# A mixer kernel in which TensorE's waits stand one product earlier, and two small blocks of other engines move

## What is computed

```python
x = x + mamba2(xn) + ffn(xn)
# mamba2: proj = xn @ in_proj_w.T            -> gate (8192), hs|B|C (8192+1024+1024), dt (128)
#         hs,B,C = silu(conv1d_4taps(...)+b) ; dt = softplus(dt+bias); A_cs = cumsum(-exp(A_log)*dt)
#         Y_diag = ((C B^T) * exp(segsum)) @ (hs*dt)        per 128-token chunk and head
#         states = B^T @ (hs*dt*decay), carried from chunk to chunk
#         Y_off  = (C @ prev_states) * exp(A_cs);  y = Y_diag + Y_off + D*hs
#         y*silu(gate), normalised by group of 1024 channels, @ out_proj_w.T
# ffn:    xn @ W.T + b + a low-rank term whose rank (8,16,32,64) a softmax picks per token
```

## Time and profile before

| | us |
|---|---|
| median of 3 runs | 1581.26 (1580.66 to 1581.79) |
| the profiled execution's own time | 1580.66 |
| its span in the profile | 1578.9 |
| busy: PE, DVE, ACT, POOL | 1559.5, 1414.5, 1367.7, 1291.1 |
| mean granted TensorE clock | 1.0 of full speed |

### The profile page before, as it was taken

The page is one execution under the profiler, slowest core; times in us unless marked ns, Lnnn a source line. Parts: engine busy times, 40 slices in busy tenths (PEclk is TensorE's granted clock), DMA queues, the critical chain, the costliest instruction groups (busy, mean ns, idle before and its releaser), DMA issues.

```text
span 1578.9 us, 29209 instructions
## 1 busy us (share of the span) xinstructions
PE 1559.5 (99%) x9172; PEld 1271.9 (81%) x9172; DVE 1414.5 (90%) x2343; ACT 1367.7 (87%) x2620; POOL 1291.1 (82%) x1614
## 2 busy tenths in 40 slices
PE   8999999999999999999999999999999999999998
PEld 7877888888888888887778788888888888888886
DVE  6988999999999999999979898898898888888887
ACT  4678899999999999989846899999999999999996
POOL 5549998999999998989874488778787878787786
PEclk9999999999999999999999999999999999999999
DMA  5257767676776676766614666766667667667673
GB/s 178 94 171 223 197 214 221 196 226 195 220 225 198 213 224 199 220 202 208 198 42 142 201 198 222 218 201 225 212 200 230 200 210 222 199 221 215 202 225 92
DMA packets 231754, 311.83 MB, mean 197 GB/s; under 512 B 144176, under 2 KB 160560, under 8 KB 231344
## 3 DMA queue, kind: packets, MB, share of 16 engines
q1 hardware_dynamic: 231600, 309.97, 63.9%
HBM read 240.69 MB, written 36.70 MB: 176 GB/s over the span
## 4 chain that ended last, share of the span: by engine, by line
PE 87%; DVE 5%; POOL 4%; issue 2%; ACT 1%; DMA 1%; SPq 0%; DVEq 0%; ACTq 0%; POOLq 0%
PE bg L804 21%; PE bo L975 20%; PE bt L804 12%; PE bh L804 11%; PE by L1031 7%; PE bg L1053 7%; PE bt L1018 3%; PE bh L1018 2%; PE bo L783 1%; POOL wl L631 1%; DVE cv L1085 1%; PE bo L862 1%; POOL xl L734 1%; DMA turned<-tg 1%; POOL wol L750 1%
## 5 line engine op out<-in xcount | busy, mean ns | idle before, releaser
L407 ACT ACTIVATE mt<-cs_row,cs_tok 128x128 f32<-128x128 f32 x1024 | 324.5, 390 | 0.0
L631 POOL TENSOR_TENSOR wl<-raw,wh 128x256 fp32r<-128x256 f32 x328 | 250.2, 792 | 59.1 <-ACT wh L379 59.1
L725 POOL COPY xt<-turned 128x512 uint16<-128x512 uint16 x248 | 202.3, 862 | 42.3 <-DMA turned<-tg 42.3
L716 POOL TENSOR_TENSOR mt<-mt,gt 128x256 f32<-128x256 f32 x128 | 118.0, 943 | 141.7 <-ACT mt L588 141.2
L741 POOL TENSOR_TENSOR sqa<-sqa,sq 128x256 f32<-128x256 f32 x222 | 223.7, 1027 | 1.0 <-ACT sq L561 1.0
L750 POOL TENSOR_TENSOR wol<-raw_o,woh 128x256 fp32r<-128x256 f32 x256 | 190.4, 764 | 10.5 <-ACT woh L528 10.5
L734 POOL TENSOR_TENSOR xl<-xg,xh 128x256 fp32r<-128x256 f32 x254 | 189.7, 768 | 6.0 <-ACT xh L541 6.0
L1085 DVE SCALAR_TENSOR_TENSOR cv<-bt,par_sb,cv 128x511 f32<-128x511 f32 (+2 forms) x192 | 143.7, 748 | 49.3 <-ACT cv L383 44.8
L1085 DVE SCALAR_TENSOR_TENSOR cv<-bh,par_sb,cv 128x511 f32<-128x511 f32 (+2 forms) x192 | 143.7, 748 | 35.4 <-ACT cv L383 30.9
L379 ACT ACTIVATE wh<-raw 128x1024 fp32r<-128x1024 f32 (+1 forms) x146 | 152.3, 1043 | 0.7 <-DMA raw<-in_w_dtag 0.7
L975 PE MATMUL bo<-woh,xl 128*128 128x512 f32 x508 | 149.1, 415 | 0.4 <-POOL xl L734 0.4
(11 more groups left out here) (215 smaller groups left out, 3814.7 us busy)
## 6 DMA issues: line engine op xcount, KB each, us to landing
raw<-in_w_step SPq DMA_DIRECT2D x128, 512.0 KB, 4.6
cs_row<-cs_rows SPq DMA_DIRECT2D x128, 512.0 KB, 7.0
low_parts<-wl SPq DMA_DIRECT2D x64, 512.0 KB, 5.8
raw_o<-in_w_out SPq DMA_DIRECT2D x128, 256.0 KB, 5.7
wl<-low_parts SPq DMA_DIRECT2D x64, 512.0 KB, 4.7
ec_row<-ec_rows SPq DMA_DIRECT2D x256, 96.0 KB, 5.7
raw<-in_w_bc SPq DMA_DIRECT2D x16, 512.0 KB, 3.6
acc<-in_x SPq DMA_DIRECT2D x8, 256.0 KB, 5.4
```

The lines of the kernel that those rows point to most:

```text
L407: e = act.activation(mt[:, m % 2, h, chunk(j)], cs_row[:, m % 2, h, chunk(j)], ACT.Relu, bias=cs_tok[:, j, 2 * m + h:2 * m + h + 1], scale ...
L631: e = pool.tensor_tensor(wl[:, n % 2, cols], raw[:, n % 2, cols], wh[:, n % 2, cols].bitcast(F32), ALU.subtract)
L725: e = pool.tensor_copy(to[:, half], turned[:, NJ * half:NJ * (half + 1), :])
```

## The change

**TensorE.** With `early_state`, the waits of five kinds move to stand before the last product of the kind ahead: what the states need is awaited before the fourth `wol,xh` product; the third output part's `p_xl` before the last state product; what the chunk products need before the fourth `woh,xl` product; what the sum of squares and the carried part's first product need before the eighth chunk product; the next projection's `a_wh` before the last product of the carried part. Among the carried part's needs is the second `v_s`, so its second product now waits for the fourth.

**POOL.** `add_bias` leaves iterations 2 to 5 of the loop and stands behind `split_lo` of the groups g = 4 to 7; its first call awaits `p_lo` too.

**DVE.** The second batch's statistics and norms stand ahead of the step's taps.

The core of the diff:

```diff
                 if j == 0:
                     pool.wait_ge(ld_wb, 48)
+                    pool.wait_ge(p_lo, b + 1)
                     pool.wait_ge(pv, b * PRO_DVE + PRO_DVE_LORA)
...
                     if g == 3:
                         add_ffn(b)
+                    if g >= GROUPS - NJ:
+                        add_bias(b, g - (GROUPS - NJ))
...
-                    if 2 <= m < 2 + NJ:
-                        add_bias(b, m - 2)
...
+                    def await_states():
+                        pe.wait_ge(v_xd, did(n - 1))
+                        if not by_dma(b, m - 1):
+                            pe.wait_ge(v_x, did(n - 1))
+                        if m > 2 and (m - 2) % PER_GROUP == 0:
+                            pe.wait_ge(v_ms, did((n - 2) // PER_GROUP - 1))
+                        if m == 1:
+                            pe.wait_ge(a_bt, did(b * GROUPS + (GROUPS - 1)))
+
+                    def await_chunks():
+                        pe.wait_ge(v_x, did(n - 1))
+                        pe.wait_ge(v_m, did(n - 1))
+                        if b + 1 == NB:
+                            pe.wait_ge(p_m, m)
+                        if bank_y(b, m - 1) is by:
+                            pe.wait_ge(v_xg, did(n - 2))
+
+                    def await_squares():
+                        pe.wait_ge(v_h2, did(un))
+                        pe.wait_ge(p_sqa, squares(b, m - 2))
+
+                    def await_off():
+                        pe.wait_ge(v_sg, did(min(n, b * STEPS + STEPS - 1)))
+                        pe.wait_ge(v_off, did(n - 2))
+                        pe.wait_ge(a_s1, did(n - 1))
+                        pe.wait_ge(v_s, did(n - 1, 4, 2))
...
                                 for j in range(NJ):
+                                    if then and k == ks[-1] and j == NJ - 1:
+                                        then()
...
-                            output(range(2) if early_state else range(3))
+                            if early_state:
+                                output(range(2), await_states)
+                            else:
+                                output()
...
                         for c in range(NS):
+                            if early_state and c == NS - 1:
+                                pe.wait_ge(p_xl, did(n - 2))
...
                         if early_state:
-                            output((2,))
...
+                            output((2,), await_chunks, awaited=True)
+                        else:
+                            await_chunks()
                         for j in range(NJ):
                             for h in range(2):
+                                if early_state and j == NJ - 1 and h == 1:
+                                    if ends:
+                                        await_squares()
+                                    await_off()
...
+                            if c == 1:
+                                pe.wait_ge(v_s, did(n - 1, 4, 4))
+                            if c == NS - 1 and early_state and has(m + 1):
+                                await_weights(b, step(b, m + 1))
...
+                    if b + 1 < NB and STEPS - 12 <= m < STEPS - 6:
+                        h, part_of = divmod(m - (STEPS - 12), 3)
+                        if part_of < 2:
+                            stats_of(b + 1, 2 * h + part_of)
+                        else:
+                            variance(b + 1, h)
+                    if b + 1 < NB and STEPS - NJ <= m < STEPS:
+                        norm(b + 1, m - (STEPS - NJ))
                     if has(m):
                         for k in range(1, TAPS):
                             tap(n, un, u, mine, k)
```

More of the change, by code:

```diff
@@ L791, in tokens, with await_weights, project @@
                 return lambda k: t[:, b, k, :] if j is None else t[:, b, k, chunk(j)]
-            def project(dst, b, n, kind):
+            def await_weights(b, n):
                 pe.wait_ge(a_wh, did(n))
+            def project(dst, b, n, kind, awaited=False):
+                if not awaited:
+                    await_weights(b, n)
                 for i, (w, t) in enumerate(((wh, xTh), (wh, xTl), (wl, xTh))):
@@ L934, in sum_squares, with output @@
                         return mm
-                    def output(ks=range(3)):
+                    def await_states():
[21 more added lines that the diff above has]
+                        pe.wait_ge(v_s, did(n - 1, 4, 2))
+                    def output(ks=range(3), then=None, awaited=False):
                         first, very_last = (m - 2) % PER_GROUP == 0, n - 2 == NB * STEPS - 1
@@ L970, in output @@
                                 a, c = parts[k]
-                                wait_low(k)
+                                if not awaited:
+                                    wait_low(k)
                                 for j in range(NJ):
+                                    if then and k == ks[-1] and j == NJ - 1:
+                                        then()
                                     if k == 0:
@@ L982, in _ @@
                             pe.wait_ge(v_h2, did(un - 4 + m))
-                        project(mine, b, step(b, m), 0).then_inc(t_hs, 1)
+                        project(mine, b, step(b, m), 0, awaited=m > 2).then_inc(t_hs, 1)
                         if m == 0:
@@ L1034, in _ @@
                     if ends and m < STEPS:
-                        pe.wait_ge(v_h2, did(un))
-                        pe.wait_ge(p_sqa, squares(b, m - 2))
                         sum_squares(mine, sqa).then_inc(t_ss, 1)
@@ L1045, in _ @@
                     if has(m - 1):
-                        pe.wait_ge(v_sg, did(min(n, b * STEPS + STEPS - 1)))
-                        pe.wait_ge(v_off, did(n - 2))
+                        if not early_state:
+                            await_off()
                         for c in range(NS):
-                            if c == 0:
-                                pe.wait_ge(a_s1, did(n - 1))
-                            else:
-                                pe.wait_ge(v_s, did(n - 1, 4, 2 * c))
+                            if c == 1:
+                                pe.wait_ge(v_s, did(n - 1, 4, 4))
+                            if c == NS - 1 and early_state and has(m + 1):
+                                await_weights(b, step(b, m + 1))
                             mm = pe.matmul(bg[:, chunk(c)], S[:, c, :], ct[:, g, chunk(c + 1)], start=True, stop=True)
@@ L1361, in _ @@
                             mask_scores(b, GROUPS - 1)
-                    if b + 1 < NB and STEPS - 12 <= m < STEPS - 6:
-                        h, part_of = divmod(m - (STEPS - 12), 3)
-                        if part_of < 2:
-                            stats_of(b + 1, 2 * h + part_of)
-                        else:
-                            variance(b + 1, h)
-                    if b + 1 < NB and STEPS - NJ <= m < STEPS:
-                        norm(b + 1, m - (STEPS - NJ))
                     if has(m - 1):
```

17 lines of the change are left out of this document (3 added, 14 removed).

## The result

The changed kernel takes 1605.32 us (median of 4 runs, 1603.2 to 1605.96), the kernel before 1581.06 (4 runs, 1580.66 to 1581.79): ratio 1.015, 95% interval 1.0134 to 1.0167, 24 us slower. The sign held, and the time lies in the prediction's wide range (1574 to 1608, for 8 in 10). It lies outside the band around its forecast of 1594 (1588 to 1601): the loss is nearly twice the 13 us of its sum.

A forecast was written before the change was run, and what follows sets the result against it. The prediction took TensorE to bound the kernel (PE busy 1559.5 of 1578.9 us). Its terms, 7.8 + 3.3 + 5.3 - 2.1 - 1.2 = +13.1 us on 1580.66, gave 1594 us, with 1574 to 1608 for 8 in 10.

The forecast's parts named there:

- early wait for `xd`: Wait moved before the fourth `wol,xh` product: load late, partly covered; 7.8 us in batch 0, 3.3 us in batch 1.
- early wait for `v_s`: Wait moved before the eighth chunk product: 2.0 us plus 3.3 us, sum 5.3 us, with ends of 1 and 16.
- bias and statistics: POOL's bias moved to later groups, -2.1 us; DVE's statistics moved ahead of the taps, -2.8 us.
- norm before the taps: Iteration 60, DVE: the norm waits for POOL's first `rstd`, `xd` comes 2.66 us later; +1.6 us.
- the met waits: TensorE's early `p_xl`, `v_x`, squares' waits and `a_wh`: already met when reached, so they cost nothing.
- the two gaps at the change of width: Idle "issue" before chunk (45.5 us) and carried loads (21.5 us) stays; rival blaming the waits: 1557 us, chance 0.12.
- `xd` in an ordinary step of batch 0: Fourth `wol,xh` load 0.19 us late, 0.12 free; about 0.10 us lost in each of about 46 steps.
- the step on `v_s` before the eighth chunk product: Second state sum ends 0.01 us before the last chunk load, 0.06 needed; 0.05 us for 40 steps, 2.0 us.
- the 0.10 us of credit in batch 0: The `xd` stall comes after `t_g`, so its 0.10 us was to cover the need of `v_s` in batch 0.
- a group's second step: TensorE meets DVE's late state sums one product sooner: 0.26 us more in 7 steps of batch 1.
- `xd` in batch 0: Early `xd` wait: 46 steps at 0.10 us and 14 at the full 0.23 us, 7.8 us together.
- The rival of the freed DVE: TensorE's slower pace shifts POOL's work out of `xd`'s way; `xd` terms fall to about 2 us: 1583.4, chance 0.15.

## Why the prediction came out as it did

| term, us | forecast | measured | from |
|---|---|---|---|
| early wait for `xd` | +11.1 | +7.5 | 1590.09 - 1582.58 |
| early wait for `v_s` | +5.3 | +15.2 | 1605.32 - 1590.09 |
| bias and statistics | -4.9 | -3.5 | 1577.89 - 1581.35 |
| norm before the taps | +1.6 | +3.5 | 1582.58 - 1579.06 |
| the met waits | 0 | +1.2, not told from 0 | 1579.06 - 1577.89 |

The differences hold in this order only, and each is uncertain by some 2 us. Without the wait for `xd`, the one for `v_s` costs 20.7 us (1603.32 - 1582.58), for then nothing covers part of it. The two together cost 22.7 us, and the forecast for them was 16.4. That is 6.3 of the missing 11 us; the norm, the smaller gain of bias and statistics and the met waits are the rest.

**What held.** The bound and the mechanism: TensorE sets the pace, the two gaps at the change of width do not come from the waits, and each early wait costs what it is late, less what is covered. The rule of the Trainium skill (TensorEngine Tiling (Array Packing), Key Properties), that a change of tiling mode drains TensorE, agrees with the rows: in the kernel before, the changed one and the two with met waits alone they have 45.5 to 47.1 us of "issue" at the chunk loads and 21.5 to 22.5 at the carried part's, whichever waits stood there. `xd` in an ordinary step of batch 0 was right to the hundredth: 0.22 lost, 0.12 given back; and in batch 1 the version with `v_s` late again pays 3.3 to 3.5 us, forecast 3.3. By the starts of the states' loads the bias gave 2.0 us up to the sixth, forecast 2.1, and the statistics 2.9 from the 52nd to the 59th, forecast 2.8; the medians show 3.5 of these 4.9, which their spread allows.

**What failed: the step on `v_s` before the eighth chunk product.** The prediction set the second sum's end (1127.24) against the last chunk load (1127.25) and took 0.05 us for 40 steps. Three things were wrong in it. The wait sits on the first of the product's two loads, which runs at 1127.14, beside the seventh product's. The release takes 0.10 us, not 0.06, as four semaphores meet there. Then the load is 1127.24 + 0.11 - 1127.14 = 0.21 us late, of which 0.05 is covered: 0.16, the measured 0.157. Against the kernel before, a step of batch 1 is 0.166 us longer (10.946, before 10.780). Third, the 0.10 us of credit in batch 0 did not cover the need: without the `xd` stall the chunk loads are 0.21 us longer there, the stall covers 0.11, and 0.10 is left to pay in each step. The prediction had 5.3 us for all of `v_s`. By the starts of the states' loads the changed kernel takes 7.5 us more than the one with `v_s` late again in the first 58 steps of batch 0 and 7.1 in batch 1. In batch 1 an ordinary step pays 0.09 net, as the 0.07 of `xd` goes away at the same time, and a group's second step 0.38 (11.15 to 11.53), where the prediction had 0.26. The prediction named both of the first two ("if the four semaphores need an extra instruction and the wait reaches the first of the product's two loads") and gave 16 us as the upper end, but took a value near the lower one. The row with four loads in 0.25 us, which shows the pairs, stood in the same trace.

**`xd` in batch 0** was put too high, and this hid part of the error on `v_s`. The forecast was 7.8 us, of which 3.2 for 14 steps at the full 0.23: the second and third of each group. With `v_s` late again, against the version with only met waits, the first 58 steps take 3.7 us more, and the 23 of them at the starts of groups only 0.6 together, though TensorE waits for `xd` there in both. So such a step did not lose the 0.23; why not, no run here settles. The 7.5 us of the table also hold 1.3 us around iteration 60, where one profile has 6.8 us at half clock and the other 3.4.

**The norm** was forecast to delay `xd` by 2.66 us and to cost 1.6. DVE stood 2.66 instead of 2.2, and `xd` behind it took 1.10 us instead of 0.55, since it met other work of POOL than before. And the sum had no term for the clock, which fell to half for 3.4 us behind the wait.

**The rival of the freed DVE** was half right: in batch 1 `xd` fell from 772 to 603 ns, and its term there vanished. But the time did not fall, since the stall that freed it cost more. That rival's sum puts the `v_s` term at 4 where the text has 5.3; with 5.3 it gives 1584.7 and not 1583.4.

## What to carry to other kernels

Before a wait is moved ahead, set the end of what it waits for against the start of the very instruction that will carry it, the first load of the product, in a window narrow enough to part loads that run in pairs. Add the release time, which depends on how many semaphores meet there: a late one is worth keeping apart from met ones. A met wait cost nothing in any place tried here, so moving it brought nothing; and a stall may show only as longer busy time of a group, never as a wait. Where an engine stands for microseconds, look at the granted clock behind it too.

## What the hardware showed that I had not expected

**`xd` finishes 0.41 us after a POOL instruction.** POOL's subtraction for `xl`, two instructions, and DVE's `xd` in four kernels, batch 1. The kernel before:

```profile
1122.51 1.45 POOL L734 TENSOR_TENSOR xl<-xg,xh 128x256 fp32r<-128x256 f32 x2
1123.56 0.81 DVE L1299 TENSOR_TENSOR xd<-xt,dd_tok 128x384 f32<-128x384 f32 x1
```

The changed one:

```profile
1117.76 1.43 POOL L737 TENSOR_TENSOR xl<-xg,xh 128x256 fp32r<-128x256 f32 x2
...
1119.01 0.60 DVE L1333 TENSOR_TENSOR xd<-xt,dd_tok 128x384 f32<-128x384 f32 x1
```

The one with the state sums awaited late:

```profile
1130.61 1.44 POOL L737 TENSOR_TENSOR xl<-xg,xh 128x256 fp32r<-128x256 f32 x2
1131.49 0.97 DVE L1336 TENSOR_TENSOR xd<-xt,dd_tok 128x384 f32<-128x384 f32 x1
```

The one with the state copy first:

```profile
1112.62 1.44 POOL L737 TENSOR_TENSOR xl<-xg,xh 128x256 fp32r<-128x256 f32 x2
1113.62 0.85 DVE L1333 TENSOR_TENSOR xd<-xt,dd_tok 128x384 f32<-128x384 f32 x1
```

`xd` lies beside the end of `xl` for 0.40, 0.18, 0.56 and 0.44 us, and lasts 0.81, 0.60, 0.97 and 0.85: the difference is 0.41 or 0.42 each time. POOL's other work does the same. In batch 0 nearly half of them begin beside the sum of squares (L741) instead and end 0.42 us after the end of its first instruction. In the fourteen profiles, from 150 us to 1575 us, 1622 of 1709 `xd` end between 0.400 and 0.425 us after the end of some POOL instruction. The other 87 all last 0.545 to 0.557 us, the least there is. So what one shape takes here, from 0.55 to 1.19 us, goes with where in POOL's work `xd` begins. The Trainium skill (SBUF — State Buffer, SBUF: two separate sides) describes such a lock, held for a whole instruction; the rows agree. No run here moved POOL's work alone.

**The granted clock can fall behind a wait.** Eight of these kernels have the norm ahead of the taps with a late `rstd`. In the profiles of seven of them TensorE's loads stand 2.5 to 4.1 us for `xd` of iteration 60, and the granted clock is 0.5 for 3.4 or 6.8 us, from within the wait or from up to 1.2 us behind it; in the eighth they stand 3.2 us and it stays at 1.0. None of the six other kernels has such a stretch. With the state sums awaited late again, the one execution with a mean granted clock of 1.0 took 1586.02 us, the four with 0.998 took 1589.49 to 1591.15.

**Two products with 64 weight columns load together.** Their loads start in pairs, 0.10 to 0.11 us apart, and a stall on one of them shows as 16.8 us more busy time in the group rather than as idle time. **One semaphore releases a load in 0.04 us, several in 0.10**; the second was seen in 96 of 97 steps of the changed kernel, the first in 58 of 59 steps of batch 1 with `v_s` alone.
